# One more pair between rounding and value products in the attention loop of a transformer tower

## The reference, cut to what matters

```python
# four layers ("banded" in the kernel)
scores = jnp.einsum('bhcqd,bhckd->bhcqk', qc, kb) / jnp.sqrt(jnp.asarray(d, q.dtype))
scores = jnp.where(allowed, scores, jnp.asarray(-1000000000.0, scores.dtype))   # |rel| <= 64
probs = jax.nn.softmax(scores, axis=-1)
out = jnp.einsum('bhcqk,bhckd->bhcqd', probs, vb)
...
# the fifth attention (not banded), B, S = x.shape[:2]
attn = jnp.einsum('bhqd,bhkd->bhqk', q, k) * SCALE
attn = jax.nn.softmax(attn, axis=-1)
out = jnp.einsum('bhqk,bhkd->bhqd', attn, v)
```

## Time and profile before

| | |
|---|---|
| time, median of 3 runs | 1869.17 us (1867.4 to 1871.43) |
| the profiled execution, its span | 1874.5 us |
| busy: TensorE (PE) | 1483.1 us, 79% |
| busy: VectorE (DVE) | 1247.8 us, 67% |
| busy: ScalarE (ACT) | 977.2 us, 52% |
| busy: GpSimd (POOL) | 808.0 us, 43% |
| line 685, ScalarE, exponentials | 406.9 us, 960 instructions |
| line 799, VectorE, low parts | 275.5 us, 480 instructions |
| line 792, VectorE, maxima | 274.3 us, 480 instructions |
| line 698, ScalarE, high parts | 244.3 us, 480 instructions |

### The profile page before, as it was taken

One profiled execution on the slowest core, in us unless ns is written; L12 is line 12 of the kernel. 1 busy time (PEld: TensorE's weight loads), 2 busy tenths in 40 slices (PEclk: granted clock), 3 DMA queues, 4 the chain that ended last, 5 costly groups with the idle time before them and its releaser, 6 DMA issues.

```text
span 1874.5 us, 42615 instructions
## 1 busy us (share of the span) xinstructions
PE 1483.1 (79%) x13098; PEld 1235.0 (66%) x13098; DVE 1247.8 (67%) x3542; ACT 977.2 (52%) x2392; POOL 808.0 (43%) x1177
## 2 busy tenths in 40 slices
PE   0589889798897997998988759759668887499992
PEld 0367678677676776776767648449646766389992
DVE  4788966788767888668896652433379896434344
ACT  0378733688434885348873223225348882155550
POOL 6577333684235762247733310124356521144440
PEclk9899989899899997999998968669869996599996
DMA  4666101743005550035610000147534511257765
GB/s 105 176 149 127 36 1 33 170 86 84 1 5 138 108 121 2 1 70 140 128 33 1 1 14 1 45 138 224 173 89 100 112 22 45 97 175 237 225 212 179
DMA packets 144317, 178.26 MB, mean 95 GB/s; under 512 B 22096, under 2 KB 106128, under 8 KB 143952
## 3 DMA queue, kind: packets, MB, share of 16 engines
q1 hardware_dynamic: 136784, 158.18, 32.9%
q0 software_dynamic: 7296, 17.18, 2.8%
HBM read 132.96 MB, written 42.34 MB: 94 GB/s over the span
## 4 chain that ended last, share of the span: by engine, by line
PE 31%; DVE 14%; issue 4%; DMA 2%; ACT 2%; POOL 2%; SPq 0%; DVEq 0%; POOLq 0%; ACTq 0%
PE bank L1473 7%; DVE ptl L799 4%; PE bank L1459 2%; DVE neg_max L792 2%; PE bank L645 1%; DVE xn L912 1%; PE bank L563 1%; PE bank L1460 1%; PE bank L1463 1%; PE bank L1461 1%; PE bank L1462 1%; PE bank L1217 1%; DMA xn<-y_rows 1%; PE bank L431 1%; PE bank L584 1%
## 5 line engine op out<-in xcount | busy, mean ns | idle before, releaser
L685 ACT ACTIVATE prob<-bank,neg_max 128x192 f32<-128x192 f32 (+1 forms) x960 | 406.9, 437 | 109.3 <-DVE neg_max L792 97.0
L792 DVE TENSOR_REDUCE neg_max<-bank 128x2 f32<-128x384 f32 (+1 forms) x480 | 274.3, 572 | 99.0 <-PE bank L544 91.4
L799 DVE TENSOR_TENSOR ptl<-bank,pth 128x384 f16<-128x384 f32 (+1 forms) x480 | 275.5, 574 | 4.6 <-ACT pth L698 4.0
L563 PE MATMUL bank<-ident,prob 128*128 128x128 f32 x1536 | 268.4, 288 | 0.0
L698 ACT ACTIVATE pth<-bank 128x384 f16<-128x384 f32 (+1 forms) x480 | 244.3, 509 | 9.3 <-PE bank L563 9.2
L652 ACT ACTIVATE xx<-bank 128x256 fp32r<-128x256 f32 x256 | 95.5, 386 | 196.0 <-PE bank L431 192.0
L544 PE MATMUL bank<-kx,qx 96*128 96x192 bf16 (+1 forms) x960 | 168.1, 257 | 1.1 <-DVE xx L766 1.1
L563 PEld LDWEIGHTS bank<-ident,prob 128*128 128x128 f32 x1536 | 162.9, 143 | 0.1
L584 PE MATMUL bank<-v,pth 128*128 128x33 bf16 x1152 | 138.4, 180 | 21.2 <-DVE ptl L799 18.0
L645 PE MATMUL bank<-w,fbuf 128*128 128x192 f32 x768 | 140.7, 327 | 2.0 <-DVE h L889 2.0
L734 ACT ACTIVATE fbuf<-bank,b 128x512 f32<-128x512 f32 x96 | 65.8, 687 | 146.5 <-PE bank L453 146.4
(11 more groups left out here) (295 smaller groups left out, 4522.5 us busy)
## 6 DMA issues: line engine op xcount, KB each, us to landing
xn<-in_e_seg SPq DMA_DIRECT2D x34, 768.0 KB
w<-in_e_w SPq DMA_DIRECT2D x23, 576.0 KB
qk_rows<-fbuf SPq DMA_DIRECT2D x128, 96.0 KB, 2.3
qx<-qk_rows SPq DMA_DIRECT2D x35, 288.0 KB, 4.0
kx<-qk_rows SPq DMA_DIRECT2D x35, 288.0 KB, 5.8
qk_rows<-w SPq DMA_DIRECT2D x80, 96.0 KB, 2.3
qx<-qk_rows SPq DMA_DIRECT2D x35, 192.0 KB, 4.6
kx<-qk_rows SPq DMA_DIRECT2D x35, 192.0 KB, 5.2
```

Source lines behind the costliest of these rows:

```text
L563: last = nc.tensor.transpose(bank[BT[p % 2]][:, c * P:c * P + P], probs_at(p, banded, c * P, P), ident[:, :])
L685: nc.scalar.activation(probs_at(p, banded, qt * n, n), scores_at(p, n)[:, qt, :], ACT.Exp, bias=neg_max[:, b % 2, hd, qt:qt + 1], scale=1. ...
L792: nc.vector.tensor_reduce(neg_max[:, b % 2, hd, :], scores_at(p, D if banded else S), AX.X, ALU.max, negate=True).then_inc(max_ready.sem, 1)
L799: nc.vector.tensor_tensor(ptl[:, p % 2, 0:n], bank[BT[p % 2]][:, 0:n], pth[:, p % 3, 0:n], ALU.subtract)\
```

## The change

On TensorE the transposes of pair p-3 come first in an iteration, then the scores of the next pair, p+1, then the value products of pair p-5, then the step; S(0) stands ahead of the loop. On ScalarE H(p-3) comes ahead of both halves of E(p). On VectorE the low part is that of pair p-3 in place of p-4. To make room, `pth` has a fourth buffer and `ptl` a third one, both in unused bytes of `fbuf`, and the two waits for free buffers are one pair looser.

```diff
+        spare_f16 = [flat(fbuf[:, 2 * j:2 * j + 2, :], "p a n -> p (a n)")[:, 3 * GW // 2:2 * GW].bitcast(F16) for j in range(2)]
+        pth_at = [pth[:, j, :] for j in range(3)] + [spare_f16[0]]
+        ptl_at = [ptl[:, j, :] for j in range(2)] + [spare_f16[1]]
...
-                nc.tensor.matmul(o, pth[:, p % 3, w], v[sums], start=first, stop=False)
...
+                nc.tensor.matmul(o, pth_at[p % 4][:, w], v[sums], start=first, stop=False)
...
+            pe_scores(pe, it, 0, banded)
             for p in range(PAIRS + 5):
-                if p < PAIRS:
-                    pe_scores(pe, it, p, banded)
-                if p >= 5:
-                    pe_values(pe, it, p - 5, banded)
                 if p == 3:
                     pe.wait_ge(y_read.sem, y_read.at(it, 0))
                 if 0 <= p - 3 < PAIRS:
                     pe_turn_probs(pe, it, p - 3, banded)
+                if p + 1 < PAIRS:
+                    pe_scores(pe, it, p + 1, banded)
+                if p >= 5:
+                    pe_values(pe, it, p - 5, banded)
                 pe_step(pe, it, p, banded, w, w_out, tile, xx)
...
         def act_hi(act, it, p, banded):
-            act.wait_ge(pv_done.sem, pv_done.at(it, p - 2))
+            act.wait_ge(pv_done.sem, pv_done.at(it, p - 3))
...
             for p in range(PAIRS + 3):
-                if p < PAIRS:
-                    act_exp(act, it, 2 * p, banded)
                 if 0 <= p - 3 < PAIRS:
                     act_hi(act, it, p - 3, banded)
                 if p < PAIRS:
+                    act_exp(act, it, 2 * p, banded)
                     act_exp(act, it, 2 * p + 1, banded)
...
         def dve_lo(dve, it, p, banded):
-            dve.wait_ge(pv_done.sem, pv_done.at(it, p - 1))
+            dve.wait_ge(pv_done.sem, pv_done.at(it, p - 2))
...
-                if 0 <= p - 4 < PAIRS:
-                    dve_lo(dve, it, p - 4, banded)
+                if 0 <= p - 3 < PAIRS:
+                    dve_lo(dve, it, p - 3, banded)
```

More of the change, by code:

```diff
@@ L583, in product @@
                 third = (slice(None),) * (len(v.shape) - 1) + (slice(1 + DH, OC),)
-                nc.tensor.matmul(o, pth[:, p % 3, w], v[sums], start=first, stop=False)
-                nc.tensor.matmul(o[third], pth[:, p % 3, w], v[lows], start=False, stop=False)
-                return nc.tensor.matmul(o, ptl[:, p % 2, w], v[sums], start=False, stop=stop)
+                nc.tensor.matmul(o, pth_at[p % 4][:, w], v[sums], start=first, stop=False)
+                nc.tensor.matmul(o[third], pth_at[p % 4][:, w], v[lows], start=False, stop=False)
+                return nc.tensor.matmul(o, ptl_at[p % 3][:, w], v[sums], start=False, stop=stop)
             if banded:
@@ L695, in act_hi @@
             act.wait_ge(t_done.sem, t_done.at(it, p + 1))
-            act.wait_ge(pv_done.sem, pv_done.at(it, p - 2))
+            act.wait_ge(pv_done.sem, pv_done.at(it, p - 3))
             n = turns(banded) * P
-            nc.scalar.activation(pth[:, p % 3, 0:n], bank[BT[p % 2]][:, 0:n], ACT.Copy).then_inc(hi_ready.sem, 1)
+            nc.scalar.activation(pth_at[p % 4][:, 0:n], bank[BT[p % 2]][:, 0:n], ACT.Copy).then_inc(hi_ready.sem, 1)
         def act_open(act, it, kind, i, banded, tile):
@@ L796, in dve_lo @@
             dve.wait_ge(hi_ready.sem, hi_ready.at(it, p + 1))
-            dve.wait_ge(pv_done.sem, pv_done.at(it, p - 1))
+            dve.wait_ge(pv_done.sem, pv_done.at(it, p - 2))
             n = turns(banded) * P
-            nc.vector.tensor_tensor(ptl[:, p % 2, 0:n], bank[BT[p % 2]][:, 0:n], pth[:, p % 3, 0:n], ALU.subtract)\
+            nc.vector.tensor_tensor(ptl_at[p % 3][:, 0:n], bank[BT[p % 2]][:, 0:n], pth_at[p % 4][:, 0:n], ALU.subtract)\
                 .then_inc(lo_ready.sem, 1)
```

## The result

The changed kernel takes 1895.49 us, the median of four runs (1893.16 to 1902.29), against 1870.3 of the kernel before (1867.4 to 1873.98). The ratio is 1.0141, with a 95% interval from 1.0117 to 1.0165: 1.4% slower, where I had forecast 0.8%.

What follows compares the result with a forecast made beforehand. The prediction took a TensorE-VectorE chain to bound the kernel, replaced by a ScalarE-VectorE chain. Four banded layers +10 and the fifth attention +4.7 us gave +15: profiled 1874.5 to 1889.5, median 1884, range 1874 to 1896.

Steps and rivals of the forecast that it cites:

- The chain between ScalarE and VectorE: In the attentions: maximum, both exponentials, step, high part, low part, next-but-one maximum; 2.20 us per two banded pairs, 2.67 in the fifth.
- the one between TensorE and VectorE: Chain binding the old attentions; cutting it should mostly remove value products' 163.0 us and maxima's 91.4 us waits.
- Quarters by counting: Chain price plus extras per attention quarter; second layer: second +0.3, third -1.5, last +2.0 us against before.
- the other turn: Alternate turn of the two-pair chain, holding reciprocals and a small exponential; 0.3 us a quarter, 1.2 for four.
- First quarters: Start of each attention, with start-up and norm work not priced; +1 us each, out of 0 to +2.5.
- the turn of the extras: The one of two alternating chain turns where steps and finishes all fall; a finish there costs 0.73 us, banded.
- The last quarter: Last 23 pairs of each attention: +2.0 us in banded layers (34.2 against 32.15), +2.1 in the fifth.
- The ends: Behind each attention's last maximum, one low part fewer: -0.5 us, between -0.9 and 0.
- Rival 1: In the attentions, the gain arrives and VectorE's own work is the floor: -45 us, 1824; chance 0.13.
- Rival 2: Over the attentions, first- and last-quarter losses hide and third quarters gain: about 1871 us; chance 0.11 together with rival 4.
- rival 4: In the attentions, loops of the two other engines stay coupled; same time as Rival 2, chance 0.11 together.
- Rival 3: On TensorE, transposes behind chunk steps hold up high and low parts: 25 us on top, 1909; chance 0.06.

## Why the forecast was right in kind and short in size

- **The chain between ScalarE and VectorE takes the place of the one between TensorE and VectorE: shown.** V hardly waits for the low part any more (3.7 us) nor M for scores (10.1); the low part waits 104.8 us for the high part (forecast 80 to 120, but "in more than half of the pairs" was wrong: 203 of 480). With the low part four behind, line 802 waits for high parts 1.9 us in all, and the kernel is 1% faster than before. But there M waits 80.6 us for scores again: that this wait vanishes by itself, as the forecast had it, is not so. It is short in the changed kernel because the new chain is the slower one.
- **Quarters by counting.** Second layer: second quarter forecast 35.3, measured 36.26; third 33.1, measured 33.63; last 34.2, measured 35.02. Fifth attention: 40.1, 37.3 and 32.9, measured 41.6, 37.4 and 32.4. Each sign is right. To the banded ones 0.3 was to be added for the other turn; measured 0.5 to 1.0. In the turn read off above 0.11 us were missing, 0.08 of them in the two exponentials; twelve such turns would make 1.3 us, more than was measured, so not every turn is like it, and how the excess divides between the two turns is open.
- **First quarters: the mis-sized term.** Forecast +1 each (and 0.3), measured +14.4 for the five. The sum took them at a guess out of 0 to +2.5, without pricing the norm work, and even that end was too low: the mean is +2.9. Norm work of the banded layers, which fell into the turn of the extras, is 5.0 of the 10.9 us that their first quarters lost; the early L(0) is a part of the rest, and what else is in it stays open.
- **The last quarter.** +2.0 was forecast against the second layer's. Over the five it is +10.4 measured, 10.1 forecast. But in the kernel before the first and third layer's last quarters had been at a granted clock of 0.95 and took 33.6 and 33.3 us, not 32.2, so a second layer of before was no fair sample. That the sum over the five agrees is in part luck: in the second layer +2.9 was measured, and the fifth attention gave +1.7 in place of +2.1.
- **The ends.** Forecast -0.5 each, measured -5.5 for the five, -1.1 each, beyond the bound of -0.9.
- **Together** the forecast terms make +14.7, the measured ones +23.4: first quarters +7.9, the other fifteen +3.8, the ends -3.0. Outside the attentions the span is 2 us shorter. The measured median, 1895.49 us, is only 0.5 us inside the forecast's own range of 1874 to 1896, and that is partly luck: the ends gave back 3 us more than forecast, and without these it would lie outside.
- **Rival 1, the gain arrives: refuted for the change, and true of its TensorE part alone,** at 20 us in place of 45. The Trainium skill, "Perfetto Trace Analysis", section "Identifying Performance Opportunities", says that a gap that repeats can mean too few buffers; here it did not mean that, since two more buffers alone gave 0.9988, no difference.
- **Rival 2, it cancels out, and rival 4, only the names of waits change: refuted** by +1.4% and by the 104.8 us.
- **Rival 3, T behind the chunk step holds up H and L: refuted.** Line 702 waited for transposes 11.0 us in all (4.9 into `pth` and 6.1 into `fbuf`; 9.2 before); it was to be over 30.

## What to carry to other kernels

Count the chain that the new order makes and not only the one that it cuts: write down for each instruction what its engine does ahead of it, and look for the way back to the same engine after one or two turns. A step that alternates between odd and even turns costs by the turn it stands in; moving one into the other turn gave 0.7% here. If a reordering has several parts, time them apart and in pairs: here TensorE's order with the buffers took 1% off, the buffers and ScalarE's order did nothing alone, and the earlier low part cost 2.5% with ScalarE's order and some 20% without it.

## What the runs showed of the hardware

**A late load is paid twice, the second time at half clock.** In the kernel with the low part four behind, first layer, TensorE stood idle from 150.5 to 153.6 us (3.1 us) for the k rows of the next entries. Two-microsecond windows of TensorE from there (busy, granted clock):

```profile
154.00:156.00 2.00, 2.00 (x22) 0.50 1.07 201
156.00:158.00 2.00, 2.00 (x14) 0.50 0.23 52
158.00:160.00 2.00, 2.00 (x20) 0.72 0.00 0
160.00:162.00 2.00, 2.00 (x21) 1.00 0.04 8
```

In the second layer the same wait was 0.95 us, and the clock stayed up:

```profile
402.00:404.00 2.00, 1.04 (x15) 1.00 1.04 185
404.00:406.00 2.00, 2.00 (x30) 1.00 1.06 234
```

0.50 is the lower of the two levels, 1.2 GHz. The first layer's third quarter, from the first maximum behind the wait on, took 34.3 us, the second layer's 32.1: 2.2 us on top of the wait. The third and fourth layers' took 34.7 and 34.1 at a clock of 0.92 and 0.93. With TensorE's order alone the same quarter shows it by layers (window, length, busy, pairs, clock):

```profile
154.57:189.68 35.11, 13.15 (x24) 0.93 0.51 104
402.55:435.28 32.73, 13.08 (x24) 1.00 0.60 121
649.16:681.88 32.72, 13.06 (x24) 1.00 0.57 120
890.54:924.52 33.98, 13.12 (x24) 0.95 0.57 119
```

In the changed kernel these quarters of the banded layers, and their second and last ones, stood at 1.00 in all four layers: its chain is slower, the loads are in time, and the clock holds. The two quarters below 1.00 above are 3.6 us longer together than two at 1.00, so the clock is likely one reason why cutting the chain brought less than expected; no run changes the clock alone.

**A VectorE instruction beside a GpSimd one.** Line 860 on VectorE started at 354.28 and ended at 355.53; it took 1.25 us, where the shortest of that line took 0.34. GpSimd's row beside it:

```profile
354.11 1.26 POOL L1064 TENSOR_TENSOR qf<-qf,w 128x512 f32<-128x512 f32 x1 [0.18 <-POOL w L1063]
```

It ended at 355.37, so most of the 1.25 us seems to have been waiting for it. Three instructions later line 851 took 1.32 us, from 356.38, beside GpSimd's line 1066 from 356.33 to 357.49; at 352.08 it had taken 0.41. The Trainium skill, "GPSIMD Engine Reference", section "Specifications", says that GpSimd shares its interface to SBUF with VectorE and contends with instructions that have two SBUF inputs; line 860 has two, and by that rule the trace agrees. Summed over the banded layers the norm work took 47.1 us in the kernel before and 47.0 in the changed one, and 37.0 and 37.2 where it was moved ahead of the loop. So it costs both kernels the same busy time, and it can add to the loss only because in the changed kernel it stands where the chain binds.
